# Feed-forward net of a graph network: gate and up products in three sums over three shared PSUM banks, nine products a matrix in place of ten

## The reference

```
def _quantize_weight(w, group_size):            # group_size = 128
    wg = w.reshape(o, i // group_size, group_size)
    scale = jnp.mean(jnp.abs(wg), axis=-1, keepdims=True) + EPS
    return (jnp.clip(jnp.round(wg / scale), -1.0, 1.0) * scale).reshape(o, i)

gate = _bitlinear(x, w_gate)      # (6250, 512) by (1408, 512)
up = _bitlinear(x, w_up)
h = jax.nn.silu(gate) * up
return _bitlinear(h, w_down)      # (6250, 1408) by (512, 1408)
```

## Time and profile before

| | us |
|---|---|
| median of 3 runs | 3246.15 (3240.7 to 3249.64) |
| profiled execution | 3251.79 |
| its span, first to last instruction | 3250.0 |
| mean granted TensorE clock over the span | 0.929 of full speed |
| stage of the feed-forward net (block C) | about 663 to 1915 |

### The profile page before, as it was taken

How to read it: one execution, slowest core, us unless ns; L and a number is a source line. 1 busy time by engine, 2 the same in 40 slices (tenths; PEclk the granted TensorE clock), 3 DMA queues, 4 the chain that set the end, 5 groups by cost and what they waited for, 6 DMA issues and landing times. The chain is left out here.

```text
span 3250.0 us, 59097 instructions
## 1 busy us (share of the span) xinstructions
PE 2693.1 (83%) x16318; PEld 1942.7 (60%) x16319; DVE 1886.2 (58%) x3394; ACT 1259.4 (39%) x2019; POOL 1891.1 (58%) x1940
## 2 busy tenths in 40 slices
PE   7789865579998989898999957778787887878799
PEld 7779864457777777777777743334343333435577
DVE  7679777646665565666666553333434444443687
ACT  2288643334544445444444440111222121214454
POOL 1077770577777777777400017777776767771465
PEclk9999985689999999999999978989999999998799
DMA  6354530213333333333323347777777877775574
GB/s 225 120 140 121 126 84 3 63 36 98 97 84 102 98 113 87 107 98 107 93 80 101 97 147 219 226 232 220 235 244 231 246 227 240 243 234 170 172 242 145
DMA packets 239794, 483.61 MB, mean 149 GB/s; under 512 B 75343, under 2 KB 92969, under 8 KB 239535
## 3 DMA queue, kind: packets, MB, share of 16 engines
q0 software_dynamic: 103936, 233.92, 26.6%
q1 hardware_dynamic: 135598, 246.49, 23.2%
HBM read 413.43 MB, written 73.35 MB: 150 GB/s over the span
## 5 line engine op out<-in xcount | busy, mean ns | idle before, releaser
L1975 POOL DMA_INDIRECT rows<-xn_rows,srcT x784 | 743.1, 948 | 273.0 <-issue 239.4
L132 POOL DMA_INDIRECT msg_c<-hid_rows,srcT x744 | 755.0, 1015 | 241.8 <-issue 225.7
L2114 PE MATMUL pV<-rows,oh 128*128 x2240 | 557.8, 398 | 145.0 <-DVE oh L2409 48.8
L1492 PE MATMUL gates<-xT,wgu_hi 128*128 128x384 f32 (+1 forms) x1848 | 481.5, 383 | 42.5 <-ACT gate_sum L1590 21.6
L2114 PEld LDWEIGHTS pV<-rows,oh 128*128 x2240 | 225.2, 101 | 463.4 <-issue 291.2
L1523 PE MATMUL accs<-wd,hT 128*128 128x512 f32 x1617 | 403.9, 397 | 15.9 <-DVE hT L1738 15.9
L1492 PEld LDWEIGHTS gates<-xT,wgu_hi 128*128 128x128 f32 x1848 | 343.1, 194 | 111.1 <-issue 65.8
L1523 PEld LDWEIGHTS accs<-wd,hT 128*128 128x128 f32 x1617 | 301.8, 188 | 87.7 <-issue 27.9
L2409 DVE SCALAR_TENSOR_TENSOR oh<-ids,bases,dstT 128x896 f32 x160 | 184.1, 1150 | 227.4 <-issue 164.0
L2397 DVE TENSOR_TENSOR agg<-agg,pV x161 | 110.1, 684 | 320.9 <-PE pV L2114 320.3
L132 POOL DMA_INDIRECT msg_b<-hid_rows,srcT x240 | 242.3, 1010 | 76.2 <-issue 72.0
(11 more groups left out here) (426 smaller groups left out, 4525.0 us busy)
## 6 DMA issues: line engine op xcount, KB each, us to landing
wd<-wd_rows SPq DMA_DIRECT2D x154, 512.0 KB
lo<-lo_rows SPq DMA_DIRECT2D x68, 256.0 KB, 3.4
we<-in_L_ffn_expert_w SPq DMA_DIRECT2D x16, 1024.0 KB
x_rows<-xr SPq DMA_DIRECT2D x49, 256.0 KB, 4.3
xn_rows<-pair SPq DMA_DIRECT2D x49, 256.0 KB, 2.2
rows<-xn_rows,srcT POOLq DMA_INDIRECT x784
res<-x_rows SPq DMA_DIRECT2D x49, 256.0 KB, 3.9
x_rows<-agg SPq DMA_DIRECT2D x49, 256.0 KB, 4.1
```

Of the source, the lines that this page charges most:

```text
L132: nc.gpsimd.indirect_dma_start(msg[:, c, :], None, table, bass.IndirectOffsetOnAxis(ap=srcT[:, c:c + 1], axis=0)).then_inc(landed[u % 2], 16)
L1492: last = nc.tensor.matmul(ps[:, 0:n], w, v, start=(m == 0), stop=(m == len(terms) - 1))
L1975: nc.gpsimd.indirect_dma_start(rows[:, u % RING, c, :], None, xn2_rows, bass.IndirectOffsetOnAxis(ap=srcT[:, u * Q + c:u * Q + c + 1], axi ...
L2114: last = nc.tensor.matmul(pV[:, ds(to, 1), :].rearrange("p a d -> p (a d)"), oh[:, ds(to, 1), c, :].rearrange("p a d -> p (a d)"), rows[:, ...
```

## The change

The four input blocks of a matrix go into three sums: block 0 alone, block 1 alone, and blocks 2 and 3 together, the fourth with the ratio of scales and its rest as before. That is two, two and five products: nine a matrix, eighteen a step. The three sums of the gate stand in three banks, and the three of up in the same three, in the same order (`ring`). ScalarE drains the first sum of each matrix, VectorE the second and the third, so VectorE has two draining instructions a matrix. Each sum of up now waits for the gate sum of the same step in its bank, and each gate sum for the up sum of the step before. In block B the ratio is formed for one input block a matrix, not two, and `wodd` and `wgu_lo` are half as wide.

```
-        wgu_lo = sb(ffn, "wgu_lo", [P, 2 * FB, DK // 2, P], F32R)
-        wscale = sb(ffn, "wscale", [P, 2 * FB, DK // 2], F32)
+        wgu_lo = sb(ffn, "wgu_lo", [P, 2 * FB, 1, P], F32R)
+        wscale = sb(ffn, "wscale", [P, 2 * FB, SP], F32)          # SP = 3
...
-            pU = [pb(ctx, "pU0", [P, 4 * P], F32), pG[0]]
+            pU = [pb(ctx, "pU0", [P, 4 * P], F32)]
+            ring = [pG[0], pG[1], pU[0]]
+            gate_at = [ring[e % 3] for e in range(SP)]
+            up_at = [ring[(SP + e) % 3] for e in range(SP)]
...  TensorE
-                    a, b = 2 * e, 2 * e + 1
-                    terms = ((hi[:, a, :], x_hi[:, a, :]), (hi[:, a, :], x_lo[:, a, :]), (hi[:, b, :], x_hi[:, b, :]),
-                             (hi[:, b, :], x_lo[:, b, :]), (lo[:, e, :], x_hi[:, b, :]))
+                    terms = [(hi[:, e, :], x_hi[:, e, :]), (hi[:, e, :], x_lo[:, e, :])]
+                    if e == SP - 1:
+                        terms += [(hi[:, 3, :], x_hi[:, 3, :]), (hi[:, 3, :], x_lo[:, 3, :]), (lo, x_hi[:, 3, :])]
...
-                    wait_alone(pe, s["up_b"], step + 1, s["fence_pe"])
-                    hidden(pG[0], g, f, 0, 0).then_inc(s["gate_ps"], 1)
-                    wait_alone(pe, s["gate_b"], step + 1, s["fence_pe"])
-                    hidden(pG[1], g, f, 0, 1).then_inc(s["gate_ps"], 1)
+                    wait_alone(pe, s["up_a"], step + 1, s["fence_pe"])
+                    hidden(gate_at[0], g, f, 0, 0).then_inc(s["gate_ps"], 1)
+                    wait_alone(pe, s["up_b"], 2 * step + 1, s["fence_pe"])
+                    hidden(gate_at[1], g, f, 0, 1).then_inc(s["gate_ps"], 1)
+                    wait_alone(pe, s["up_b"], 2 * step + 2, s["fence_pe"])
+                    hidden(gate_at[2], g, f, 0, 2).then_inc(s["gate_ps"], 1)
...
-                    wait_alone(pe, s["up_a"], step + 1, s["fence_pe"])
-                    hidden(pU[0], g, f, 1, 0).then_inc(s["up_ps"], 1)
                     wait_alone(pe, s["gate_a"], step + 1, s["fence_pe"])
-                    hidden(pU[1], g, f, 1, 1).then_inc(s["up_ps"], 1)
+                    hidden(up_at[0], g, f, 1, 0).then_inc(s["up_ps"], 1)
+                    wait_alone(pe, s["gate_b"], 2 * step + 1, s["fence_pe"])
+                    hidden(up_at[1], g, f, 1, 1).then_inc(s["up_ps"], 1)
+                    wait_alone(pe, s["gate_b"], 2 * step + 2, s["fence_pe"])
+                    hidden(up_at[2], g, f, 1, 2).then_inc(s["up_ps"], 1)
...  VectorE, gate (up is alike)
-                    dve.wait_ge(s["gate_ps"], 2 * step + 2)
                     dve.wait_ge(s["gate_a"], step + 1)
-                    nc.vector.scalar_tensor_tensor(gate_sum[:, 0:n], pG[1][:, 0:n], wscale[:, f, 1:2], gate_sum[:, 0:n],
-                                                   ALU.mult, ALU.add).then_inc(s["gate_b"], 1)
+                    for e in range(1, SP):
+                        dve.wait_ge(s["gate_ps"], SP * step + (e + 1))
+                        if e > 1:
+                            dve.wait_ge(s["gate_b"], (SP - 1) * step + (e - 1))
+                        nc.vector.scalar_tensor_tensor(gate_sum[:, 0:n], gate_at[e][:, 0:n], wscale[:, f, e:e + 1], gate_sum[:, 0:n],
+                                                       ALU.mult, ALU.add).then_inc(s["gate_b"], 1)
```

More of the change, by code:

```diff
@@ L43 @@
 M = 136
+SP = 3
 MB = 4
@@ L825, in program @@
             wthree = sb(weights, "wthree", [P, 2 * DK, P], BF16)
-            wodd = sb(weights, "wodd", [P, DK, P], F32)
+            wodd = sb(weights, "wodd", [P, 2, P], F32)
             wdraw = sb(weights, "wdraw", [P, FB, P], F32)
@@ L948, in wide @@
                     quantize(wsize[:], wsign[:], wthree[:], 2 * DK, s["signs"], f + 1)
[L949 to L955, removed]
+                    scales = sc[:, 1, 0:2 * DK].rearrange("p (k e) -> p k e", k=2)
+                    ratio = sc[:, 3, 0:2]
+                    nc.vector.tensor_copy(wscale[:].rearrange("p (k f) e -> p k f e", k=2)[:, :, f, :], scales[:, :, 0:SP])
+                    own.step(nc.vector.reciprocal(ratio, scales[:, :, 2]))
+                    own.step(nc.vector.tensor_mul(ratio, scales[:, :, 3], ratio))
+                    nc.vector.tensor_tensor(wodd[:], wthree[:].rearrange("p (k e) c -> p k e c", k=2)[:, :, 3, :],
+                                            bc(ratio.unsqueeze(2), (P, 2, P)), ALU.mult).then_inc(s["wq"], 1)
                     dve.wait_ge(s["wq"], f + 1)
@@ L959, in wide_rest @@
                     dve.wait_ge(s["hi"], f + 1)
[L960 to L963, removed]
+                    nc.vector.tensor_tensor(wgu_lo[:].rearrange("p (k f) e c -> p k f (e c)", k=2)[:, :, f], pW[:, :, 3, :],
+                                            wgu_hi[:].rearrange("p (k f) a c -> p k f a c", k=2)[:, :, f, 3, :].bitcast(F32),
+                                            ALU.subtract).then_inc(s["lo_done"], 1)
                 def down(i):
@@ L1213, in wide @@
                     for j in range(2):
-                        for e in range(DK // 2):
-                            nc.tensor.matmul(pW[:, j, 2 * e, :], wthree[:, j * DK + 2 * e, :], identb[:], start=True, stop=True)
-                            last = nc.tensor.transpose(pW[:, j, 2 * e + 1, :], wodd[:, j * DK // 2 + e, :], ident[:])
+                        for e in range(SP):
+                            last = nc.tensor.matmul(pW[:, j, e, :], wthree[:, j * DK + e, :], identb[:], start=True, stop=True)
+                        last = nc.tensor.transpose(pW[:, j, 3, :], wodd[:, j, :], ident[:])
                     last.then_inc(s["ps"], 1)
@@ L1421, in _ @@
             def _(pe):
-                for n in ("used", "silu", "hmul", "xT_lo", "gate_b", "up_a", "up_b"):
+                for n in ("used", "silu", "hmul", "xT_lo", "up_a"):
                     pe.sem_inc(s[n], 1)
+                pe.sem_inc(s["up_b"], SP - 1)
                 pe.sem_inc(s["down"], 2)
@@ L1588, in gate @@
                     act.wait_ge(s["silu"], step + 1)
-                    act.wait_ge(s["gate_ps"], 2 * step + 1)
-                    nc.scalar.activation(gate_sum[:, 0:n], pG[0][:, 0:n], ACT.Identity, scale=wscale[:, f, 0:1]).then_inc(s["gate_a"], 1)
+                    act.wait_ge(s["gate_ps"], SP * step + 1)
+                    nc.scalar.activation(gate_sum[:, 0:n], gate_at[0][:, 0:n], ACT.Identity, scale=wscale[:, f, 0:1]).then_inc(s["gate_a"], 1)
                 def up(i, g, f):
```

18 lines of the change are left out of this document (11 added, 7 removed).

## The result

The changed kernel took 3375.71 us in the median (3369.06 to 3380.09), the kernel before, run beside it, 3243.43: a ratio of 1.0407, with a 95% interval of 1.0377 to 1.0437, so about 132 us slower where 138 were forecast. Its profiled execution took 3369.06 us, with a span of 3367.3.

A forecast was written before the change was run, and what follows sets the result against it. TensorE was taken to bound the stage of the net, busy 1145 of 1252 us. The terms -63 + 46 + 85 + 32 + 75 - 56 + 22 - 3 = +138 on 3246 gave 3384 us, range 3310 to 3440.

The forecast's parts named there:

- Part 1: Stage of the net: two products fewer in each of 154 steps, 63 us gained if TensorE stays the bound.
- Part 2: Up's third sum waits for the gate's third drain: 0.25 us (512 columns) or 0.35 (384) a step, 46 us lost.
- Part 3: Up's second sum waits behind VectorE's long jobs: 85 us lost at `build`, 32 at `stats`, 75 in groups' first steps.
- Part 4: TensorE's waits for late ScalarE work, and half of that for a group's last `low`, go: 56 us back.
- Part 5: Slow clock behind half of TensorE's stalls of 2 us or more: 22 us lost (0 to 65).
- the clock rival: All 51 long stalls of TensorE, not half, are followed by slow products: 43 us more, 3427 us; chance 0.10.
- Part 6: Block B: `wodd` and the subtraction for `wgu_lo` halved on VectorE, 3 us gained (0 to 7.6).
- a walk of part 3: Step-by-step timing of VectorE and TensorE around a long job; 192 us over 58 long places, mean stall 3.3 us.
- the length of the stage: Sign for the whole stage of the net: some 135 us longer; no longer than 1252 us would be wrong.

The follow-up runs named there:

- e1: The kernel before, with nine products a matrix in its two sums and its old banks: 3210.15 us, ratio 0.9899.
- e4: The changed kernel, with up's sum of five products moved ahead of its other two: 3334.99 us, ratio 1.0289 to the kernel before.
- e5: The kernel before, with nine products a matrix and two more drain-shaped VectorE instructions a step on SBUF, ahead of the drains' waits: 3281.88 us, ratio 1.0114.
- e6: The changed kernel, with the two products of up's first sum issued six times in the long-wait steps: 3355.51 us, ratio 1.0358 to the kernel before.

## Why the prediction was right, and where not

The total was right (+132 against +138), in part by luck: the products gained 30 us less than forecast, and load and ring together cost 70 + 95 = 165 us where parts 2 to 6 gave 46 + 192 - 56 + 22 - 3 = 201. The place was right too, the steps with VectorE's long jobs: steps 0 to 4 and 7 of the two groups grew by 9.8 + 10.2 us a turn, some 140 in seven turns, while all others together shrank by 0.4 us a turn. The split among causes was not right.

- **Part 1, the products: mis-sized.** Forecast 63, measured 33 (e1). It stood on "if TensorE stays the bound", and I read that from a share of 1145 of 1252 us. In steps 1 to 4 of each group TensorE was not the bound (VectorE stands behind it for 0.3 us in all there); there two products less are worth nothing, some 23 of the missing 30 us (7 x 4 x 0.47 and 7 x 4 x 0.35).
- **Part 2, U2's wait: right in a plain step, its total not shown.** Forecast 0.25 and 0.35 us a step, measured 0.33 and 0.48 in steps without other work. The short term was the hand-over to VectorE, which I put at 0.05 us; with 512 columns it is 0.13. In 154 steps that would be 62 for my 46, but with 384 columns most steps have other products between G2 and U0 that cover it: in step 10 of six turns U0 to `down` takes 1.68 to 1.72 us, some 0.1 over the nine products. And e4, which takes this wait away, gave 38 in all, shorter long waits among them. By the rule of the Trainium skill weighed there (Perfetto Trace Analysis, section Matmuls) the rotation would have hidden the drain; the trace does not bear that out for four products between drain and reuse, and does for seven (e4).
- **Part 3, the long jobs: places right, sizes too large in the first step, the cause half of it.** Leaving out the first turn's two, the stalls after a `build` were 1.66 to 3.93 us with 384 columns (forecast 2.7 and 3.3), 0.60 to 2.38 and 1.96 to 2.47 with 512 (2.6 and 2.1); after `stats` 1.22 to 1.52 with 512 and 3.06 to 3.46 with 384 (1.86 and 3.15); at U1 behind `stats_rows` 2.77 to 2.80 and 3.38 to 3.91 (4.65 and 5.2). They add up to some 141 us for my 192. The step that failed is another: I charged VectorE's extra drains only where the ring makes TensorE wait for them, since "Before, TensorE asks VectorE for drains of the step before", and so at nothing with the old banks. But two more instructions a step cost 70 us with the old banks (e5), mainly in steps whose pace VectorE's own row of work sets. From e1 to e5 TensorE's waits for ScalarE's `gate_sum` and `xn` grow by 13.5 and 12.7 us, those for VectorE's `up_sum` by 17.1. The ring itself cost 95, in place of the 46 + 192 - 56 = 182 that parts 2 to 4 gave it.
- **Part 4, the waits that go: right in direction.** The waits for `aggT` and for the `xn` of the earlier trace rows are gone, ScalarE's `gate_sum` fell from 21.2 to 11.5, and `hT` from 14.8 to 8.2, near the half that I forecast.
- **Part 5, the clock: right in direction, its worth in time not isolated.** The stage fell from 0.97 to 0.93. Between the levels of 2.4 and 1.2 GHz that is 14% of 1384 us, 194 us, at the lower, against 75 before, so some 60 us of work, where I forecast 22. I took half of the long stalls as followed by a slow stretch; of the 43 waits of 2.26 us and more for VectorE's `gate_sum`, 41 were, with 0.56 to 0.79 in the 7 us behind them. So the clock rival had the right condition, and yet not its time: filling the waits, which brought the clock back, gave only 16 us net (e6). That much of the slow work fills time in which TensorE would wait anyway fits this, but no run shows it apart from what the added products cost.
- **Part 6, block B: too small to tell.** The net's first gate product came at 655.4 to 661.4 us in the five kernels with the new weights, at 654.2 to 663.6 in the eight with the old ones; the means are 1.6 us apart, less than either spread.

The first step of a group in the changed kernel, on the timeline of both engines:

```profile
1172.26 2.46 DVE L1694 BATCH_NORM_STATS2 small<-xr 128x6 f32<-128x512 f32 x4
...
1175.95 0.62 DVE L1733 SCALAR_TENSOR_TENSOR gate_sum<-gates,wscale,gate_sum 128x384 f32<-128x384 f32 x1 [0.25 <-DVE small L1700]
...
1176.71 0.98 PE L1496 MATMUL gates<-xT,wgu_hi 128*128 128x384 f32 x2 [3.65 <-DVE gate_sum L1733]
```

The reader should see the same shape as at the `build`: the long job, the drain, the product 0.14 us behind it.

Of the signs that I named, the busy time of VectorE (959.94 for 960), the clock under 0.97 and the length of the stage came as told. The wait for VectorE's `gate_sum` was 159.4 us in all, not 200, and that the longest was over 4 us is luck: the two that are lie in the first turn, behind GpSimd, and the longest that a walk of part 3 describes is 3.93.

Still open is how the ring's 95 us divide among the short wait at U2, the long ones and the slow clock, and whether the load would cost the same with drains that read PSUM: the two instructions of e5 read SBUF. The shares are differences of runs with intervals of 0.5 to 1.2% from end to end, so 33, 70 and 95 are good to some 20 us each.

## What to carry to other kernels

Before crediting fewer matmuls, ask in each kind of step whether TensorE paces it: a busy share of nine tenths held stretches where two products less gave nothing and two VectorE instructions more, on an engine 60% busy, cost 0.75 to 0.95 us in most steps. Look at what the other engine waits for there: VectorE stood behind TensorE for 0.3 us in 56 steps, so its own row set the pace. When sums share banks, count from the end of a sum's last product to the reuse of its bank (landing, hand-over, drain, release), put the longest sum into that gap, and look for what else the draining engine may have begun by then. A right total can hide wrong shares, so run each part of a change by itself.

## What the runs showed of the hardware

In the changed kernel the clock fell after long waits and not with short ones. In the 7 us after the wait of 3.93 us the granted clock was 0.56. Of the waits for VectorE's `gate_sum`, the 18 of 0.5 to 1.96 us had 1.00 in the 7 us behind them, and the 43 of 2.26 us and more 0.56 to 0.79, save two of 2.38 and 2.47 us that had 1.00, both in the first stretch shown. In the stretches whose plain steps have U2's waits of 0.33 and 0.48 us it stayed at 1.00 (from 1085 and from 2020 us). The rule of the Trainium skill that short idle times between groups can make the clock swing (TensorE: Matmul & The Clock Gate, section A second HAM failure mode: psum-queue depth-cycling) is thus not what this kernel shows. And a clock brought back from 0.93 to 0.98 by added products came with only 16 us less (e6). From the end of a sum's last product to VectorE's drain of it 0.13 us passed, from the drain's end to the product that it released 0.15 (the step from 1106.43 us).
